# Moving the preparation of the first layer's feed-forward weights from a stage of its own into the first slots of the pipeline

## What is computed

```
def fp4_quant_dequant(x):
    xb = x.reshape(shape[:-1] + (shape[-1] // 16, 16))
    scale = max(max(abs(xb), axis=-1) / 6.0, 1e-12)
    q = nearest(GRID, abs(xb / scale)) * sign(xb) * scale   # GRID = 0, .5, 1, 1.5, 2, 3, 4, 6

def ffn(x):                       # w_gate, w_up: (704, 256), w_down: (256, 704)
    gate = fp4(x) @ fp4(w_gate).T
    y    = fp4(x) @ fp4(w_up).T
    h    = silu(gate) * y
    return fp4(h) @ fp4(w_down).T

h = layernorm(pairs(x) @ conv_w + conv_b + mean(pairs(x))) * gamma + beta
h = h + attention(layernorm(h));  h = h + ffn(layernorm(h))
h = layer1(h)                     # untouched by the change
```

## Time and profile before

| | us |
|---|---|
| median of 3 executions | 4659.44 |
| lowest and highest | 4658.25, 4665.62 |
| the profiled execution, by the clock of the device | 4667.47 |
| its span in the trace, first to last instruction | 4665.6 |
| mean granted TensorE clock, as a share of full | 0.985 |

### The profile page before, as it was taken

One profiled execution on the slowest core, in us unless ns is written; L12 is line 12 of the kernel. 1 busy time (PEld: TensorE's weight loads), 2 busy tenths in 40 slices (PEclk: granted clock), 3 DMA queues, 4 the chain that ended last, 5 costly groups with the idle time before them and its releaser, 6 DMA issues.

```text
span 4665.6 us, 119233 instructions
## 1 busy us (share of the span) xinstructions
PE 4432.7 (95%) x43016; PEld 3952.5 (85%) x43016; DVE 3333.5 (71%) x6915; ACT 2640.0 (57%) x5596; POOL 1959.1 (42%) x2582
## 2 busy tenths in 40 slices
PE   3999999999999985999999999999999999999997
PEld 2888888888888864899999999999999999998986
DVE  4888888888888863566666666666666666666665
ACT  2666666666666643455555555555555555555553
POOL 1455555555555531334334334334334334334333
PEclk9999999999999997999999999999999999999998
DMA  2000000000000001000000000000000000000000
GB/s 84 20 24 20 24 24 24 22 22 24 24 24 21 23 15 39 8 8 8 15 9 8 15 9 8 15 9 8 15 9 8 15 9 8 15 9 8 15 5 11
DMA packets 64945, 79.30 MB, mean 17 GB/s; under 512 B 8758, under 2 KB 51126, under 8 KB 64438
## 3 DMA queue, kind: packets, MB, share of 16 engines
q1 hardware_dynamic: 64566, 74.07, 5.4%
HBM read 49.40 MB, written 24.64 MB: 16 GB/s over the span
## 4 chain that ended last, share of the span: by engine, by line
PE 56%; DVE 2%; issue 1%; ACT 1%; POOL 1%; DMA 0%; ACTq 0%; DVEq 0%; SPq 0%; POOLq 0%
PE bA L938 11%; PE bA L939 9%; PE bA L940 9%; PE bS L1223 4%; PE bO L1245 3%; PE bA L1307 3%; PE bB L938 2%; PE bB L1208 2%; PE bB L1209 2%; PE bB L940 2%; PE bB L939 2%; PE bA L1308 2%; PE bT L1261 2%; PE bO L1254 1%; PE bO L1249 1%
## 5 line engine op out<-in xcount | busy, mean ns | idle before, releaser
L1638 POOL TENSOR_TENSOR sqs_lo<-sq,sqs_hi 128x768 fp32r<-128x768 f32 x256 | 477.9, 1867 | 676.7 <-ACT sqs_hi L1358 673.1
L1449 DVE TENSOR_TENSOR qk_lo<-bA,qk_hi 128x384 fp32r<-128x384 f32 x512 | 284.5, 556 | 538.6 <-ACT qk_hi L1358 538.5
L1377 ACT ACTIVATE phi<-bB 128x768 f32<-128x768 f32 x256 | 207.4, 810 | 665.1 <-PE bB L1209 665.1
L1596 POOL TENSOR_TENSOR yT_lo<-tanh_y,yT_hi 128x384 fp32r<-128x384 f32 x256 | 259.4, 1014 | 556.8 <-ACT yT_hi L1358 556.8
L1358 ACT ACTIVATE qk_hi<-bA 128x384 fp32r<-128x384 f32 x512 | 251.6, 491 | 203.7 <-PE bA L940 203.5
L1459 DVE TENSOR_TENSOR aT<-bS,mask 128x1024 f32<-128x1024 f32 x256 | 311.0, 1215 | 2.0 <-PE bS L1228 1.3
L1367 ACT ACTIVATE sq<-bA 128x384 f32<-128x384 f32 x512 | 250.3, 489 | 62.0 <-DVE qk_lo L1449 61.8
L518 PE MATMUL bank<-down_sb,hqT 128*128 128x256 f32 x1128 | 278.7, 389 | 1.0 <-ACT hqT L600 1.0
L616 ACT ACTIVATE kblk<-gu,kb_masked,rowmask 128x128 f32<-128x128 f32 x752 | 271.3, 463 | 8.1 <-PE gu L542 8.1
L518 PEld LDWEIGHTS bank<-down_sb,hqT 128*128 128x128 f32 x1128 | 204.3, 190 | 52.8 <-issue 32.6
L938 PE MATMUL bA<-fc_lo,yT_hi 128*128 128x256 f32 x768 | 230.6, 300 | 12.9 <-ACT pre L1407 6.2
(11 more groups left out here) (245 smaller groups left out, 15104.2 us busy)
## 6 DMA issues: line engine op xcount, KB each, us to landing
xT<-in_x SPq DMA_DIRECT2D x94, 256.0 KB, 2.6
h_scratch<-h SPq DMA_DIRECT2D x188, 64.0 KB, 1.9
hx<-h_scratch SPq DMA_DIRECT2D x32, 256.0 KB, 2.7
out<-res SPq DMA_DIRECT2D x32, 256.0 KB, 2.2
hx<-h_scratch SPq DMA_DIRECT2D x64, 64.0 KB, 2.5
out<-res SPq DMA_DIRECT2D x64, 60.0 KB, 1.8
q<-in_fc_q SPq DMA_DIRECT2D x2, 1024.0 KB, 6.4
wq_sb<-in_wq SPq DMA_DIRECT2D x1, 1024.0 KB, 5.0
```

The source lines that it names most:

```text
L1449: dve.tensor_tensor(dst, src, hi.bitcast(fp32), ALU.subtract).then_inc(S[done], 1)
L1638: pool.tensor_tensor(sqs[1][:], sq[:], sqs[0][:].bitcast(fp32), ALU.subtract).then_inc(S["sq_lo"], 1)
```

## The change

The weight stage with its block and barrier is gone, and with it `fp4_round` and `fp4_quantize`. Gate and up lie in SBUF as `[128, 6, 256]` (the last group half filled and padded with zeros). `slots` calls `weights(t)` on each engine ahead of each unrolled slot, and further pieces stand inside the slots:

- SP issues conv weights, the first tile of x, gate, the small vectors, q, k, v, out, up, down; layer 1's four weights follow ahead of slot 5.
- DVE: scales of gate ahead of slot 0; in slot 0 the addition of the value bias, scales of up, rounding of gate; in slot 1 rounding of up and scales of down; in slot 2 the low parts of gate and of up; at the end of slot 2 rounding of down.
- POOL does the multiplications: gate and up scaled in slot 0, gate's values ahead of slot 1, up's values and down scaled in slot 1, down's values ahead of slot 3.
- ACT makes the magnitudes: of gate in slot 0 behind `ln1_copy`, of up at the end of slot 0, of down at the end of slot 2; the high parts in slot 2, the copies of down in slot 4.
- PE makes the value bias product ahead of `qk_product(0)` in bank `sc`. It transposes gate and up in slot 2 and down in slot 4, in groups of three into one half (one bank) of `pt` each, four groups for each matrix.

```
-SCALE_OPS, ROUND_OPS, ROUND2_OPS = 4, 4, 2
-FP4_OPS = SCALE_OPS + 1 + ROUND_OPS + 1
+SCALE_OPS, ROUND2_OPS = 4, 2
...
-        with ExitStack() as tmp:
...
+        wraw = {"gate": sb("graw", [128, GROUPS, DM]), "up": sb("uraw", [128, GROUPS, DM]), "down": sb("draw", [128, KC, F0])}
...
@@ slots
             for t in range(first):
+                weights(t)
                 slot(t, t % 2)
@@ SP
-                load(0, 0)
+                def weights(t):
+                    if t == 0:
+                        sp.dma_start(conv_sb[:], conv_w.rearrange("(c p) n -> p c n", p=128)).then_inc(wconv, 16)
+                        load(0, 0)
+                        for n, src in (("gate", gate_w), ("up", up_w)):
...
+                    if t == 5:
+                        for dst, v in (("wq_sb", wq), ("wk_sb", wk), ("wv_sb", wv), ("wo_sb", wo)):
+                            sp.dma_start(w1[dst][:], v.rearrange("(c p) n -> p c n", p=128)).then_inc(w1_loaded, 16)
@@ PE
                 def gate(t, r):
+                    if isinstance(t, int) and t == 3 and r == 0:
+                        pe.wait_ge(wlow, 8)
...
                 def hq_transpose(t):
+                    if isinstance(t, int) and t == 4:
+                        pe.wait_ge(wdown, 6)
...
                 def p_transpose(t):
+                    if isinstance(t, int) and t == 2:
+                        pe.wait_ge(wlow, 8)
...
                 def qk_product(t):
+                    if isinstance(t, int) and t == 0:
+                        value_bias()
+                        pe.wait_ge(wqkv, 16 * 3)
...
                         scores(t)
+                    if isinstance(t, int) and t == 2:
+                        weight_jobs("gate")
+                    if isinstance(t, int) and t == 4:
+                        down_jobs()
...
                         outproj(t)
+                    if isinstance(t, int) and t == 2:
+                        weight_jobs("up")
...
-                pe.wait_ge(wfold, 6 + 2 * KC)
-                pe.wait_ge(wcopied, len(JOBS))
-                pe.wait_ge(wlow, 2)
+                def weight_rows(n, c, h):
+                    for j in range(3 * h, 3 * h + 3):
+                        rows = 128 if j < GROUPS - 1 else LAST
+                        o = 128 * (j - 3 * h)
+                        last = pe.transpose(pt[:, h, o:o + rows], wraw[n][0:rows, j, 128 * c:128 * (c + 1)],
+                                            ident[0:rows, 0:rows])
+                    last.then_inc(wtrans, 1)
+                def weight_jobs(n):
+                    i = ("gate", "up").index(n)
+                    pe.wait_ge(W[n]["ready"], 1)
+                    pe.wait_ge(S["PT_copied"], 1)
+                    for k in range(2 * KC):
+                        if 4 * i + k >= 2:
+                            pe.wait_ge(wlow, 4 * i + k - 1)
+                        weight_rows(n, k // 2, k % 2)
...
@@ ACT slot: ln1_copy, then
+                    if isinstance(t, int) and t == 0:
+                        weight_magnitude("gate")
@@ ACT slot: behind v_copy
+                    if isinstance(t, int) and t == 2:
+                        weight_high("gate")
+                    if isinstance(t, int) and t == 4:
+                        down_copy()
@@ ACT slot: behind exponentials and tanh, ahead of ln1_normalize
+                    if isinstance(t, int) and t == 2:
+                        weight_high("up")
@@ ACT slot: behind k_copy and q_copy, the last of the slot
+                    if isinstance(t, int) and t == 0:
+                        weight_magnitude("up")
+                    if isinstance(t, int) and t == 2:
+                        weight_magnitude("down")
...
+                def weight_magnitude(n):
+                    act.wait_ge(W[n]["scaled"], 1)
+                    act.activation(wmag[n][:], wflat[n], ACT.Abs, scale=SLOPE).then_inc(W[n]["abs"], 1)
@@ DVE slot: behind row_moments(y_st, 0), ahead of score_max
+                    if isinstance(t, int) and t == 2:
+                        weight_low("gate")
@@ DVE slot: behind ln0_statistics and its row_moments
+                    if isinstance(t, int) and t == 0:
+                        dve.wait_ge(wout, 32)
+                        dve.wait_ge(vbias, 1)
+                        dve.tensor_tensor(outb_bc[:], outb_bc[:], sc[:, 0, 0:DM], ALU.add).then_inc(wfold, 1)
+                        weight_scales("up", 2)
+                        weight_round("gate")
+                    if isinstance(t, int) and t == 1:
+                        dve.wait_ge(S["rs1"], 4 * 2)
+                        weight_round("up")
+                        weight_scales("down", 1)
@@ DVE slot: behind row_moments(h_st, 2), ahead of xq_scales
+                    if isinstance(t, int) and t == 2:
+                        weight_low("up")
@@ DVE slot: behind att_divide
+                    if isinstance(t, int) and t == 2:
+                        weight_round("down")
...
+                def weight_round(n):
+                    dve.wait_ge(W[n]["abs"], 1)
+                    st = Steps(dve, W[n]["round"], 0, ROUND2_OPS)
+                    fp4_round2(dve, st, wflat[n], wmag[n][:], wflat[n])
+                    st.end()
+                def weights(t):                    # DVE
+                    if t == 0:
...
+                        dve.wait_ge(wconv, 16)
...
+                        dve.wait_ge(wsmall, 16 * 6)
...
+                        weight_scales("gate", 2)
@@ POOL slot: behind rsqrt(t, 1)
+                    if isinstance(t, int) and t == 0:
+                        weight_scaled("gate")
+                        weight_scaled("up")
+                    if isinstance(t, int) and t == 1:
+                        weight_values("up")
+                        weight_scaled("down")
...
+                def weights(t):                    # POOL
...
+                    if t == 1:
+                        weight_values("gate")
+                        pool.wait_ge(wfold, 6 + 2 * KC)
+                    if t == 3:
+                        weight_values("down")
```

More of the change, by code:

```diff
@@ new lines, in layer0 @@
+        wconv, wsmall, wqkv, wout = sem("wconv"), sem("wsmall"), sem("wqkv"), sem("wout")
+        wconst, vones, wfold, vbias = sem("wconst"), sem("vones"), sem("wfold"), sem("vbias")
+        wpad, wtrans, whigh, wlow, wdown = sem("wpad"), sem("wtrans"), sem("whigh"), sem("wlow"), sem("wdown")
+        W = {n: {k: sem(f"{n}_{k}") for k in ("loaded", "scales", "scaled", "abs", "round", "ready")}
+             for n in ("gate", "up", "down")}
+        wraw = {"gate": sb("graw", [128, GROUPS, DM]), "up": sb("uraw", [128, GROUPS, DM]), "down": sb("draw", [128, KC, F0])}
@@ L354, in layer0 @@
+        wflat = {n: t[:].rearrange("p j k -> p (j k)") for n, t in wraw.items()}
+        width = {"gate": GROUPS * DM, "up": GROUPS * DM, "down": KC * F0}
+        wsmall_t = {n: sb(f"{n}_small", [128, 3, width[n] // BLOCK]) for n in wraw}
+        wmag = {n: sb(f"{n}_mag", [128, width[n]]) for n in wraw}
+        LAST = F0 - 128 * (GROUPS - 1)
         S = {n: sem(n) for n in (
@@ L388, in wait_stored, with slots @@
                 eng.wait_ge(S[f"{name}{par}"], t * 16 + (32 - 16 * par))
-        def slots(eng, slot):
+        def slots(eng, slot, weights):
             first = 6
@@ L590, in slot, with value_bias, down_jobs @@
                         pv_product(t, 1 - par)
-                pe.wait_ge(wfold, 6 + 2 * KC)
-                pe.wait_ge(wcopied, len(JOBS))
-                pe.wait_ge(wlow, 2)
-                slots(pe, slot)
+                def weight_rows(n, c, h):
[7 more added lines that the diff above has]
+                    if t == 0:
+                        pe.wait_ge(vones, 8)
+                        pe.wait_ge(wfold, 4)
+                def value_bias():
+                    pe.wait_ge(wfold, 4 + KC)
+                    pe.wait_ge(wout, 32)
+                    for c in range(KC):
+                        last = pe.matmul(sc[:, 0, 0:DM], vb_wide[:, c, :], outw_sb[:, c, :], start=c == 0, stop=c == KC - 1)
+                    last.then_inc(vbias, 1)
+                def weight_jobs(n):
[6 more added lines that the diff above has]
+                        weight_rows(n, k // 2, k % 2)
+                def down_jobs():
+                    pe.wait_ge(W["down"]["ready"], 1)
+                    pe.wait_ge(S["PT_copied"], 3)
+                    for k in range(2 * KC):
+                        c, h = k // 2, k % 2
+                        if k >= 2:
+                            pe.wait_ge(wdown, 2 * c - 1 if h == 0 else 3 * c)
+                        for f, (b, w) in list(enumerate(F0C))[3 * h:3 * h + 3]:
+                            last = pe.transpose(pt[0:w, h, 128 * (f - 3 * h):128 * (f - 3 * h + 1)],
+                                                wraw["down"][:, c, b:b + w], ident[:])
+                        last.then_inc(wtrans, 1)
+                slots(pe, slot, weights)
             @block.scalar
```

(11 more changed lines are left out.)

233 lines of the change are left out of this document (97 added, 136 removed).

## The result

The changed kernel takes 4629.93 us (median of 4 runs, 4624.68 to 4631.58) against 4658.84 (4 runs): ratio 0.9935, 95% interval 0.9917 to 0.9952, 29 us faster. The forecast was 4620, with a range from 4606 to 4637. The profiled execution took 4631.58.

The account below looks back on a forecast made before the run. Steady slots were taken as bound by PE and untouched, the first four by a chain across engines. Saved 62.8 less lost 23.5 gave net 39 us, 4620 us from a median of 4659.4, range 4606 to 4637.

Parts of the forecast that it names:

- the main case: Whole kernel: net 39 us less, 4620 us, between 4612 and 4628; chance 0.58.
- the rival with a late start: Start: small vectors land with the last transfers, y of tile 0 at 26, saving 52.8, kernel 4630; chance 0.12.
- The start: Before slot 0: vectors landed by 12.0, y of tile 0 read at 16.0 instead of 78.77, 62.8 us saved.
- Slot 0: First slot, y to y: 20.4 us instead of 15.15 through value bias, scales and gate's rounding, 5.3 lost.
- the collision: Slot 0: POOL scales up while DVE rounds gate; taken in turn, 3.0 us more.
- Slot 1: Second slot: gate's values on POOL delay `rsqrt(1, 0)` by 2.4, plus 0.3 before `att_divide`; 2.7 us lost.
- the 0.3 for `att_divide`: Slot 1: rounding up and scales of down just fit the gap before `att_divide`, 0.3 us lost.
- Slot 2: Third slot: gate's groups 4.6, up's groups 2.3, down's magnitude and rounding 5.1; 12.0 us lost, slot 28.6.
- The first 4.6: Slot 2: gate's four groups end at 6.7, so `score_max` starts there instead of at 2.13, 4.6 us lost.
- Slots 3 and 4: Values of down on POOL cost 1.0 us in slot 3; down's transpose groups cost 1.5 in slot 4.
- 1.0 for the clock: Part of slot 3 runs slower after TensorE's idling at a low clock grant: 1.0 us, bounds 0 and 5.
- layer 0's loop in another rhythm: Loop: changed arrival order and collisions; 0.45 us a slot eats the gain, one collision more per slot gives 4708; chance 0.03.

Follow-up runs that it names:

- e3_table: Changed kernel plus one tiny ScalarE Tanh activation ahead of ScalarE's first wait, so the table loads early; ratio 0.9937 to the kernel before.
- e4_no_overlap: Changed kernel with GpSimd scaling only 16 of up's 1536 columns in slot 0, computation incomplete; executed once, no ratio, slot 0 18.0 us.
- e6_down_early: Changed kernel with the early table load, and down's magnitude and rounding moved earlier in slot 2; 4618.52 us against 4662.90 before, ratio 0.9900.
- p64: Changed kernel with 64 extra, already fulfilled waits (32 instructions) in PE's idle stretch of slot 0; ratio 0.9908 to the kernel before.
- the shifted kernels: Changed kernel with 64, 128 or 192 extra fulfilled waits in PE's program in slot 0; ratios 0.9908, 0.9906 and 0.9906 to the kernel before.
- e1_repeat: Changed kernel run once more, nothing altered; 4636.74 us against 4665.67 for the kernel before, ratio 0.9938.
- the first pair: First profiles of the kernel before and the changed kernel, without further edits; medians 4658.84 and 4629.93 us, ratio 0.9935.
- p8: Changed kernel with 8 extra fulfilled waits (4 instructions) in PE's idle stretch of slot 0; ratio 0.9926 to the kernel before.
- p192: Changed kernel with 192 extra fulfilled waits (96 instructions) in PE's idle stretch of slot 0; ratio 0.9906 to the kernel before.
- p128: Changed kernel with 128 extra fulfilled waits (64 instructions) in PE's idle stretch of slot 0; ratio 0.9906 to the kernel before.

## Why the prediction was right, and where not

**The total** was right in part by luck. 4629.93 lies in the range from 4606 to 4637, but above the 4612 to 4628 of the main case and beside the 4630 of the rival with a late start, whose condition did not occur (y of tile 0 at 15.67, not 26). Layer 0 gained more than forecast, layer 1 gave back what I had put at nothing, and the range was wide enough for other reasons.

**The start** was right to 0.3 us. The small vectors had landed by 11.99, where I had 12.0; the rival with a late start is out. The 12.0 itself is two errors that cancel: by 12 us the queue had moved 2.52 MB, not 1.9, at 210 GB/s over the stretch, where I had put 158 and then 268.

**Slot 0**: 5.4 against 5.3, right by errors that cancel. I missed the load of ScalarE's table, 1.3 us. In the kernel before the load stood at 0.81 us where nobody waited; the change made ScalarE's first operation one with a wait ahead of it, and the load came behind that wait, onto the chain (shown by e3_table). Against it, the collision cost 2.5 instead of 3.0 (e4_no_overlap), POOL's multiplications 2.80 instead of 3.0, PE's value bias 1.91, and the steps overlap a little better than in my sum. What the Trainium skill says (SBUF — State Buffer, section "SBUF: two separate sides"), that an operation of VectorE with two inputs in SBUF and one of GpSimd block each other for a whole instruction, agrees with these rows in both directions: 4.24 against 1.76 on one side, 1.60 for 16 columns on the other.

**Slot 1**: 2.0 against 2.7. POOL's multiplication of gate's values was the cause (`rsqrt(1, 0)` starts at 39.78, 3.6 behind y; normally 1.3); the 0.3 for `att_divide` did not come, as y of tile 2 still waited 0.92 us for PE behind `att_divide`, and PE's k product took 1.33 us where it took 1.67 before.

**Slot 2**: 9.2 against 12.0. The three places are right (`score_max` 3.6 later, `ln1_normalize` 5.3, the rounding behind `q_copy` the rest), the sizes too large: of the four rows of six transposes three took 0.91 to 1.04 us where I had 1.44 by the low clock, and only the last took 1.62. PE was granted 0.98 between 50 and 60 us, while I had taken its idle time to keep it low; it fell to 0.50 between 65 and 70. The first 4.6 was also added up too high: my own terms, followed group by group, end at 6.3 to 6.4, not 6.7. From `ln1_normalize` to the end of `q_copy` it took 1.0 less than before, since the q and k products took 1.74 and 1.06 us instead of 1.92 and 1.91, with a clock of 0.91 between 70 and 75. That the rounding of down is a serial piece is shown by e6_down_early: without it the slot is 5 us shorter.

**Slots 3 and 4**: 1.1 and 2.3, against 1.0 and 1.5 and 1.0 for the clock. Layer 1's loads were covered, as forecast: SP's x of tile 6 was held in the queue, but y of tile 7, 17.9 us behind tile 6 in the changed kernel, is 17.3 behind it in p64, where those loads stand at the same place, so what looked like their cost belongs to the shift of PE's program.

**Layer 0 in all**: 42.9 us gained where the sum had 39.3.

**The failed step** is at the start of the working. The change "touches none of their instructions", I wrote of the steady slots of layer 0, and for those it held. But the sum has no term for layer 1 either: I put its change at nothing without a reason. By that the kernel should have been at 4616 to 4620. Layer 1 took 9.4 us longer in the mean of the profiles, and the medians of the shifted kernels are 11 to 14 us further below the kernel before than that of e1_repeat. The nearest of my rivals, layer 0's loop in another rhythm, had the kind right (a cost for each trip of a loop) but neither the loop nor the mechanism: not collisions or arrival times, but where the loop lies in PE's program. In layer 0's loop there are only the 0.6 us named above, once, and no idle time of PE beside them.

What stays open: why that place matters. A fetch of instructions in pieces would fit. The profile's instruction queue moved 4.24 MB in 259 packets, 16.4 KB each, but the trace doesn't show whether PE waited for such a piece, and I tried only five shifts. Nor is the split of the 9.4 us taken apart by an experiment. The traces do show it: in the mean, PE's idle time in layer 1 is 4.4 us longer in the bad places and its busy time, for the same 29050 matmuls, 5.0 longer, which a lower clock would explain. But it is not the same in each pair. In the first pair PE's idle time is only 1.2 longer, since PE waited 3.3 less for DVE's `xT_lo`, and its busy time 5.9 longer; and the kernel with the most issue idle, p8, doesn't have the longest layer 1. Nor do the idle times alone make the 14 to 15 us of the medians. p192's layer 1 was another 13.5 us shorter than p64's: 6.7 of it are shorter waits for `xT_lo` (16.9 and 10.2 in sum), 6.3 PE's busy time. Why is open too; its median is only 2 us lower than p128's.

## What to carry to other kernels

A stage that is dissolved into a pipeline's first slots gains what it took at the start less what each slot gets longer, and the slot's price is read off the chain: look for an engine whose next chain step stands behind the moved work, and move that work to where the engine is seen idle (5 us here). When code ahead of an unrolled loop grows or shrinks, compare the profile at the loop's back edges before judging the change: if PE idles there for nothing shown, a few dozen idle instructions ahead of it are a cheap trial. Here they were worth 11 to 14 of the 43 us that layer 0 had gained, but only 5 on top of e6's moves. Give ScalarE a dummy operation ahead of its first wait: it took 1.3 us off slot 0 here, though not clearly off the whole.

## What the runs showed of the hardware

- PE's idle time at a long loop's back edge depends on the place of the loop in PE's program: 0.3 to 1.4 us an edge in good places, 1.15 to 3.8 in bad ones, as long again in the one run with a shift by 256 instructions. TensorE's granted clock fell behind all the long ones, 2.7 us and more (0.74 from 2345 to 2350 us, behind the stall of 3.81) and behind some short ones: behind 1.17 us in the kernel before and 1.27 in p64, not behind 1.67 in the kernel after.
- GpSimd's multiplication of 16 columns took 1.60 us while VectorE worked on two SBUF operands, and VectorE's 1.76 became 4.24 beside GpSimd's multiplication of 1536 columns, which takes 2.80 alone and took 4.19 there.
- The load of ScalarE's table (1.28 us) waits with the first operation: it stood at 0.81 us where that had no wait of its own, and at 18.27 where it had.
